# Mixing the experts' weights in bf16, column tile by column tile, with two positions in one column group

## The reference, cut to what matters

```python
x = jnp.transpose(hidden_states, (1, 0, 2))       # the 112 positions come first
h = jax.nn.relu(jnp.einsum('bsh,oh->bso', x, gW1) + gb1)
gate = jnp.einsum('bsh,eh->bse', h, gW2) + gb2
g = gate.mean(axis=1)                             # 112 x 8
W1 = jnp.einsum('be,eoi->boi', g, eW1)            # 112 matrices 1024 x 256
W2 = jnp.einsum('be,eoi->boi', g, eW2)            # 112 matrices 256 x 1024
y = jax.nn.relu(jnp.einsum('bsi,boi->bso', x, W1) + (g @ eb1)[:, None, :])
y = jnp.einsum('bsi,boi->bso', y, W2) + (g @ eb2)[:, None, :]
```

## Time and profile before

| | |
|---|---|
| median of 3 runs | 985.87 us (985.53 to 988.59) |
| the profiled execution | 978.81 us |
| its span, first to last instruction | 976.9 us |
| attention | 0 to 312 us |
| gates, residual, first chunk formed and used | 312 to 411 us |
| values of chunks 1 to 30 | 411.1 to 951.4 us |
| last chunk and output | 951.5 to 976.9 us |

### The profile page before, as it was taken

One profiled execution on the slowest core, in us unless ns is written; L12 is line 12 of the kernel. 1 busy time (PEld: TensorE's weight loads), 2 busy tenths in 40 slices (PEclk: granted clock), 3 DMA queues, 4 the chain that ended last, 5 costly groups with the idle time before them and its releaser, 6 DMA issues.

```text
span 976.9 us, 31690 instructions
## 1 busy us (share of the span) xinstructions
PE 843.7 (86%) x13150; PEld 545.8 (56%) x13150; DVE 556.1 (57%) x881; ACT 552.7 (57%) x852; POOL 216.6 (22%) x406
## 2 busy tenths in 40 slices
PE   2778899999987866199999999999999999999992
PEld 2657787877865423055555555555555555555552
DVE  6666667766664323056556556556556556565561
ACT  2536666767655335065665665665665655656650
POOL 7443555545522102320020020020020020020020
PEclk9889999999999857599999999999999999999997
DMA  6468666766650794523323223332233233222103
GB/s 184 109 169 206 181 157 176 173 170 166 167 146 13 196 124 90 157 71 109 89 68 108 89 87 89 88 96 86 83 108 90 82 95 89 93 84 67 45 2 77
DMA packets 114774, 109.38 MB, mean 112 GB/s; under 512 B 13434, under 2 KB 106842, under 8 KB 114658
## 3 DMA queue, kind: packets, MB, share of 16 engines
q1 hardware_dynamic: 114658, 107.67, 42.6%
HBM read 74.73 MB, written 32.75 MB: 110 GB/s over the span
## 4 chain that ended last, share of the span: by engine, by line
PE 59%; DMA 14%; ACT 10%; SPq 6%; DVE 3%; POOL 3%; issue 3%; ACTq 0%; POOLq 0%
PE banks L1601 25%; PE banks L1618 17%; ACT wb L962 9%; DMA k_stack<-k_dram 7%; PE banks L308 4%; PE banks L1445 4%; PE banks L1339 2%; PE banks L1298 2%; PE banks L1321 2%; DMA b_dram<-b_sb 2%; SPq L431 2%; DMA b_rows<-b_dram 2%; SPq L589 1%; DMA k_dram<-k_parts 1%; POOL y L723 1%
## 5 line engine op out<-in xcount | busy, mean ns | idle before, releaser
L962 ACT ACTIVATE wb<-banks 128x896 f32<-128x896 f32 x320 | 286.5, 916 | 242.4 <-PE banks L1601 232.6
L1601 PE MATMUL banks<-spread,ring 32*128 32x448 f32 x2048 | 274.6, 606 | 60.2 <-ACT wb L962 33.3
L1185 DVE COPY wb<-banks 128x896 f32<-128x896 f32 x192 | 209.5, 1091 | 203.5 <-PE banks L1601 190.2
L1601 PEld LDWEIGHTS banks<-spread,ring 32*128 32x128 f32 x2048 | 82.7, 188 | 129.4 <-ACT wb L962 92.0
L730 POOL TENSOR_SCALAR ht<-ht 128x256 f32<-128x256 f32 x64 | 47.8, 765 | 480.8 <-DVE ht L1209 478.7
L1618 PEld LDWEIGHTS banks<-wb,xt 128*32 128x32 f32 x3584 | 91.5, 111 | 85.8 <-DVE z L1199 26.7
L1057 DVE TENSOR_REDUCE maxima<-banks 112x2 f32<-112x750 f32 x128 | 117.7, 935 | 31.8 <-PE banks L1298 28.7
L1618 PE MATMUL banks<-wb,xt 128*32 128x128 f32 x3584 | 126.3, 279 | 0.0
L1618 PEld LDWEIGHTS banks<-wb,ht 128*32 128x32 f32 x3584 | 92.2, 109 | 59.1 <-DVE y L1199 48.7
L1618 PE MATMUL banks<-wb,ht 128*32 128x128 f32 x3584 | 116.9, 275 | 0.7 <-DVE y L1199 0.5
L765 ACT ACTIVATE probs<-banks 128x448 f32<-128x448 f32 x192 | 100.6, 544 | 28.5 <-PE banks L1321 26.3
(11 more groups left out here) (122 smaller groups left out, 847.2 us busy)
## 6 DMA issues: line engine op xcount, KB each, us to landing
w_nat<-in_w SPq DMA_DIRECT2D x64, 256.0 KB, 4.4
turned_dram<-w_turned SPq DMA_DIRECT2D x32, 512.0 KB, 3.1
ring<-turned_dram SPq DMA_DIRECT2D x32, 512.0 KB, 4.0
k_dram<-k_parts SPq DMA_DIRECT2D x16, 576.0 KB, 3.6
k_stack<-k_dram SPq DMA_DIRECT2D x32, 288.0 KB
k_stack<-k_dram SPq DMA_DIRECT2D x32, 192.0 KB
c_raw<-in_ctx_t SPq DMA_DIRECT2D x16, 375.0 KB, 5.3
y<-xmid_dram SPq DMA_DIRECT2D x8, 448.0 KB, 19.2
```

The costliest lines, as they stand in the source:

```text
L962: act.activation(wb[n % 2][:, :, at:at + 8].rearrange("p b (r k) -> p b r k", r=2), banks[:, bank:bank + 2, 0:4 * NQ].rearrange("p r (b k) ...
L1185: dve.tensor_copy(wb[n % 2][:, :, at:at + 8].rearrange("p b (r k) -> p b r k", r=2), banks[:, bank:bank + 2, 0:4 * NQ].rearrange("p r (b k ...
L1601: last = pe.matmul(banks[:, form_bank(half + r // 2, r % 2), 0:4 * NQ], ring[rows, n % 2, q, :], spread[rows].rearrange("p b k -> p (b k)" ...
```

## The change: what it does

- **Bf16 products.** Each fp32 weight and each fp32 gate is split into three bf16 parts (high, middle, low). Six products of parts, 8 experts x 2 each, are stacked in K: 96 rows. A form step is now a half (16 a chunk): 16 bf16 matmuls with a stationary of 96 x 32 (32 inputs) and a moving `spread` of 112 positions x 2 outputs = 224 columns, four side by side in four column groups. They are in the same 128 x 32 column tiling as the values.
- **Splitting.** PE transposes from `w_nat` with a step of eight elements. ACT copies the half to `w_split[:, 0]` as bf16 (`turned`), DVE subtracts it from PSUM into `w_rest` (`rest`), and when both halves are there POOL copies the middle part and subtracts the low part (`split`). SP writes 768 KB (`store_split`) and reads 1,536 KB back in twelve transfers of 16 partitions and 128 KB each (`load_ring`, two parts). `w_nat`, `w_split`, `w_rest` have one slot, and `ring` is two halves of one slot.
- **Pairs.** Two positions share a column group: `xt` and `ht` have a zero pad between the first position's 16 columns and the second's, and two matmuls accumulate, so `y` and `z` have 14 groups, not 28. Four units a chunk.
- **Order.** `ORDER` puts the second layer's chunks one chunk later; `hidden` now lies among the values of the next group's first chunk, except for the last group.
- **Copies out of PSUM.** `formed` reads PSUM with the four outputs innermost, 256 columns apart; before, four neighbouring columns were innermost.
- **Bias.** The bias of the second layer is made by matmuls (`mix_b2`) while chunk 0 is formed, and DVE adds it to `y` (`add_b2`).

```diff
-        DVE_HALVES = [(1, 1, 1, 0, 1, 1, 1, 0), (1,) * 8, (1, 1, 1, 0, 1, 1, 1, 0), (1, 0, 1, 0, 1, 0, 1, 0)]
+        ORDER = [("in", 0, 0), ("in", 0, 1)]
+        for i in range(OT - 1):
+            ORDER += [("in", i + 1, 0), ("out", i, 0), ("out", i, 1), ("in", i + 1, 1)]
+        ORDER += [("out", OT - 1, 0), ("out", OT - 1, 1)]
+        SIX, SEVEN = (1, 3, 6, 9, 11, 14), (1, 3, 5, 8, 10, 12, 14)
...
+        def period(n, form, turn, hidden, value):
+            form(n + 1, 0)
+            turn(n + TURN_AHEAD, 0)
+            form(n + 1, 1)
+            turn(n + TURN_AHEAD, 1)
+            done = 2
...
+            for g in range(GRP):
...
+                if done < HALVES:
+                    form(n + 1, done)
+                    done += 1
+                if i is not None and g == 0:
+                    hidden(i, 1)
+                value(n, g)
...
+        def formed(bank):
+            return (banks[:, bank:bank + 2, :].rearrange("p a (r c) -> p (a r) c", r=2)[:, :, 0:2 * NQ]
+                    .rearrange("p r (b k) -> p b k r", k=2))
...
 # SP
+            def store_split(m):
                 if turns_alive(m):
+                    sp.wait_ge(turn_low, m + 1)
+                    sp.dma_start(split_dram[m].rearrange("c p f -> p c f"),
+                                 w_split[:].rearrange("p c q i -> p c (q i)")).then_inc(turn_stored, 16)
+            def load_ring(m, part):
                 if turns_alive(m):
                     sp.wait_ge(turn_stored, 16 * (m + 1))
+                    need(sp, form_mm, HALVES * (m - 1) + HALVES // 2 * (part + 1))
+                    for k, piece in enumerate((0, 0, 0, 1, 1, 2)):
+                        src = split_dram[m, piece].rearrange("(r s) f -> r s f", s=8)
+                        sp.dma_start(ring[2 * E * k:2 * E * k + 2 * E, 4 * part:4 * part + 4, :],
+                                     src[:, 4 * part:4 * part + 4, :]).then_inc(ring_loaded[part], 16)
...
             for n in range(CHUNKS):
-                load_ring(n + 2)
-                store_turned(n + TURN_AHEAD)
-                load_natural(n + TURN_AHEAD + 2)
+                load_natural(n + TURN_AHEAD + 1)
+                store_split(n + TURN_AHEAD)
+                load_ring(n + 2, 0)
+                load_ring(n + 2, 1)
...
 # POOL
+            def split(m):
+                if turns_alive(m):
+                    pool.wait_ge(turn_rest, 2 * m + 2)
+                    need(pool, turn_stored, 16 * m)
+                    pool.tensor_copy(w_split[:, 1], w_rest[:]).then_inc(turn_mid, 1)
+                    pool.wait_ge(turn_mid, m + 1)
+                    pool.tensor_tensor(w_split[:, 2], w_rest[:], w_split[:, 1], ALU.subtract).then_inc(turn_low, 1)
...
 # ACT
+            def turned(m, w):
+                if turns_alive(m):
+                    act.wait_ge(turn_mm, 2 * m + w + 1)
+                    need(act, turn_stored, 16 * m)
+                    act.activation(w_split[:, 0, 4 * w:4 * w + 4, :].rearrange("p q i -> p (q i)"),
+                                   banks[:, turn_bank(m, w), :], ACT.Copy).then_inc(turn_high, 1)
...
 # DVE
+            def rest(m, w):
+                if turns_alive(m):
+                    dve.wait_ge(turn_high, 2 * m + w + 1)
+                    need(dve, turn_low, m)
+                    q = slice(4 * w, 4 * w + 4)
+                    dve.tensor_tensor(w_rest[:, q, :].rearrange("p q i -> p (q i)"), banks[:, turn_bank(m, w), :],
+                                      w_split[:, 0, q, :].rearrange("p q i -> p (q i)"), ALU.subtract)\
+                        .then_inc(turn_rest, 1)
...
+            dve.wait_ge(y_loaded, 16 * 8)
+            for q in range(HALVES):
+                taken_by_dve(0, q)
+                if q % 2 == 0 and q // 2 < GRP // 2:
+                    add_b2(q // 2)
...
 # PE
+            def form(n, q):
...
+                half = HALVES * n + q
+                half_taken(half - 3)
+                if q % (HALVES // 2) == 0:
+                    pe.wait_ge(ring_loaded[q // (HALVES // 2)], 16 * PRODUCTS * (n + 1))
...
                 for r in range(4):
+                    t = 4 * q + r
+                    for j in range(4):
+                        last = pe.matmul(banks[32 * j:32 * j + 32, form_bank(half) + r // 2, 256 * (r % 2):256 * (r % 2) + 2 * NQ],
+                                         ring[0:ROWS, t // 8, P * (t % 8) + 32 * j:P * (t % 8) + 32 * j + 32],
+                                         spread[0:ROWS].rearrange("p b k -> p (b k)"), start=True, stop=True)
                 last.then_inc(form_mm, 1)
...
+                m = g - UNIT_FROM[u]
+                for h in range(2):
                     for j in range(4):
+                        if ORDER[n][0] == "in":
+                            left = xt[:, ORDER[n][2], GRP * j + g, h:h + 2, :]
+                        else:
+                            left = ht[:, 4 * g + j, h:h + 2, :]
                         last = pe.matmul(banks[32 * j:32 * j + 32, 6 + v % 2, P * m:P * m + P],
+                                         left.rearrange("p h s -> p (h s)"), wb[n % 2][:, PAIRS * h + GRP * j + g, :],
+                                         start=(h == 0), stop=(h == 1))
```

More of the change, by code:

```diff
@@ L339, in turns_alive, with hidden_before @@
             return 0 <= m < CHUNKS
[L341 to L347, removed]
+        def hidden_before(n):
+            return n >= 2 and ORDER[n - 1][0] == "in" and ORDER[n - 1][2] == 1
@@ new lines, in unit_of @@
+        def unit_of(g):
+            return max(u for u in range(UNITS) if UNIT_FROM[u] <= g)
+        def period(n, form, turn, hidden, value):
[4 more added lines that the diff above has]
+            done = 2
+            i = ORDER[n - 1][1] if hidden_before(n) else None
+            if i is not None and ORDER[n][0] == "out":
+                for u in range(UNITS):
+                    form(n + 1, done)
+                    done += 1
+                    hidden(i, u)
+                i = None
+            for g in range(GRP):
+                if i is not None and g in UNIT_FROM[:3]:
+                    hidden(i, 0 if g == 0 else UNIT_FROM.index(g) + 1)
+                if done < HALVES:
+                    form(n + 1, done)
+                    done += 1
+                if i is not None and g == 0:
+                    hidden(i, 1)
+                value(n, g)
@@ L349, in build, with number @@
         UNIT, TAKEN = {}, []
         taken = {"act": 0, "dve": 0}
-        for n in range(CHUNKS):
[L352 to L356, removed]
+        def number(key, who):
+            UNIT[key] = len(TAKEN)
+            taken[who] += 1
+            TAKEN.append((who, taken[who]))
@@ new lines, in number_turn, with number_hidden, number_value, first_half @@
+        def number_turn(m, w):
+            if turns_alive(m):
+                UNIT["turn", m, w] = len(TAKEN)
+                TAKEN.append(("turn", 2 * m + w + 1))
+        def number_hidden(i, u):
+            number(("hidden", i, u), "dve")
+        def number_value(n, g):
+            if g in UNIT_FROM:
+                number(("value", n, unit_of(g)), "act" if first_half(n) else "dve")
+        def first_half(n):
+            return ORDER[n][0] == "in" and ORDER[n][2] == 0
+        for n in range(CHUNKS):
+            period(n, lambda n, q: None, number_turn, number_hidden, number_value)
@@ L365, in turn_unit, with unit_ready @@
             return UNIT["turn", m, w]
+        def unit_ready(eng, v):
+            eng.wait_ge(unit_mm, sum(who != "turn" for who, count in TAKEN[:v + 1]))
         def unit_taken(eng, v):
@@ L1137, in step @@
                     gate_sum(3)
+                    rest(0, 0)
+                    rest(0, 1)
+                if s.i is None and s.c == B + 1:
+                    rest(1, 0)
+                    rest(1, 1)
             dve.wait_ge(ones_set, 1)
```

492 lines of the change are left out of this document (240 added, 252 removed).

## The result

The changed kernel takes 1051.99 us (median of 4 runs, 1049.67 to 1056.24), the kernel before 987.1 us beside it: ratio 1.0662, 95% interval 1.0621 to 1.0704. The forecast was 968 us with a range to 1026. The profiled execution took 1049.67 us, its span is 1047.9 us.

A forecast was written before the change was run, and what follows sets the result against it. The DRAM chain was taken to bound each chunk: 16.7 us plus surcharges 0.6 and 0.4 made 17.7. Start 390, 29 chunks, 30 and 25.5 us gave a 959 us span; adding 9, 968 us, range 907 to 1026.

The forecast's parts named there:

- PE would be done at 14.6 or earlier: PE's work in a loop chunk: forms, values, turns and hidden sum to 14.3 us, 14.6 us with a wait.
- The ring's loads: Last link of the DRAM chain: six 128 KB transfers for the ring's first part, 5.5 us, between bounds 4.6 and 6.45.
- ring loads one behind the other: Rival at `load_ring`: a ring part takes 6.45 us, 19.0 us a chunk, 1005 us in all; chance 0.27.
- The chain's links: Between successive first forms: PE, ACT and DVE to 4.4 us, POOL 7.8, store 10.9, ring part and landing 16.7.
- the rule: Partitions 0 to 15 reach four of sixteen ports, some 104 GB/s: a ring part 7.5 us, kernel some 1035 us.
- Strided PSUM reads: Rival at `formed`'s copies: ACT's 0.92 to 1.66 us, DVE's 1.09 to 2.0; 19.3 us a chunk, 1014 us; chance 0.12.
- POOL's two operations: Chain term in `split`: middle part 1.1 us and low part 2.2 us, 3.4 us with the handover.
- The store: Chain term in `store_split`: 768 KB to DRAM, 3.1 us until its packets are out.
- The start: Ahead of the loop: residual to 375 us, then 13.6 us of copies and adds; first value near 390 us (380 to 400).
- Clock: Surcharge on the chain: 0.9 us where the clock falls after a wait, at about two chunks in three, so 0.6.
- The range: Whole kernel: 15.6 to 19.6 us a chunk, 5 us either way for the start, stated as 907 to 1026 us.
- the 17.7 forecast: Time of a loop chunk: chain of 16.7 us plus surcharges of 0.6 and 0.4, against 18.0 before.

The follow-up runs named there:

- e8: The changed kernel with the edits of e5 and e4 together: half the forming instructions and, from the third chunk on, 2 of 12 ring transfers; 898.19 us.
- e4: The changed kernel with instructions as they are, but ten of the twelve ring transfers left out from the third chunk on; 963.09 us.
- e5: The changed kernel with one forming matmul over 448 columns for two weight rows, 128 instead of 256 a chunk, same tiles and transfers; 1007.46 us, ratio 1.0244.
- e3: The changed kernel with two column tiles of 64 in place of four of 32 for forming, 128 matmuls a chunk; 1005.13 us.
- e1: The changed kernel with one full-width forming matmul over 128 columns in place of four over 32, 64 instead of 256 a chunk; 1003.35 us, ratio 1.0211.
- e12: e1 plus ring rows in every sixth partition, two forms then two value groups in turn, and chunk 0 formed ahead of the bias steps; 925.68 us, ratio 0.9408.
- e15: e12 with the first half of the ring load ahead of the store of the pieces in SP's queue; 913.85 us, ratio 0.9272.
- e9: The changed kernel with the same 12 ring transfers, each into every sixth partition instead of 16 neighbouring ones; 957.85 us.

## Why the prediction was wrong, step by step

- **"PE would be done at 14.6 or earlier" was right as work and wrong as time.** This is the step that failed. I priced the 16 x 4 form groups at 0.1 us each and the values as before, and never counted what PE must be given to run them. Form groups did come 0.1 us apart, and the work is 15.0 us a chunk in e8, with half of the forming instructions, and 15.6 in e4 beside its stops. But a packet of 16 KB serves 127 records and their weight loads. Without stops, the kernel after uses one up in (506.3 - 93.4) / 97 = 4.3 us, the kernel before in 448.7 / 61 = 7.4. At 4.3 us it stops for 1.0 us on average, at 5.6 us (e5, less its waits) for 0.2, at 6.4 us and more (e3, e1, before) for 0.02 or nothing. Beside a sixth of the ring's transfers 5.3 us were enough for 0.02 (e8). No rival of mine had this mechanism; the earlier trace rows held the count from which to ask.
- **The ring's loads: the rival's size, not mine.** I took 5.5 us for half a ring with 6.45 as the bound. The packets of a half take 5.5 to 7.4 us in the kernel after, 6.2 on average. The 172 GB/s that drew me to the middle weren't k_stack's alone: of the 0.76 MB of that stretch 0.59 were. In e5, where stops take only 0.5 us a chunk, the chunk is 18.8 us: the rival *ring loads one behind the other* (19.0). The chain's links were mine in part. SP's issues for a half's first part do stand behind the store's issue, and so behind POOL, in e12 (and e15 took that link away with its wait); in e1's chain the release of the half and the store's issue end within 0.2 us of each other; and in the kernel after only 10 of 25 stood directly behind the store, the others later, where the release of the half came last, which my sum left out. There this bound is hidden behind PE's stops, so its price did not show there as a wait. It showed through the fetches.
- **The Trainium skill's SBUF — State Buffer, "Door 1: The DMA port swizzle", speaks of exactly this.** By it 16 neighbouring partitions reach four of sixteen ports. In the kernel after, the ring's packets moved 131 GB/s with all engines busy (104 by that page of the Trainium skill), and a half's 0.786 MB in 6.2 us are 126. Every sixth partition, which by the table of the same page of the Trainium skill reaches thirteen or fourteen of the sixteen ports, gave packets of 0.44 us on average instead of 0.79. The trace agrees in kind. I had used the rule as a rival at the price of the transfer alone; the placement was worth 94 us. The row of the kernel after, one microsecond inside a ring half (length, busy times, granted clock, DMA share, GB/s):

```profile
640.00:641.00 1.00, 1.00 (x42) 0.80 (x38) 1.00 (x2) 1.00 (x2) 0.00 (x0) 1.00 1.01 131
```

- **Strided PSUM reads** cost nothing: 917 and 1086 ns, as before. POOL's two operations sum to 3.2 us (forecast 3.4 with the handover), `rest` is 0.685 us (0.69). The store lands in 4.6 us; I had its packets out in 3.1.
- **The start.** The natural block came at 347.2, y at 379.9 instead of 375 (SP issued it at 361.0, not 357), and chunk 0's forming took from there to 402 instead of 13.6 us. It is PE's: at a granted clock of 0.50 four bias matmuls take 2.07 us and two halves 1.6, together 3.6 us for each of the four full rounds.

```profile
384.50 1.68 PE L1704 MATMUL banks<-spread,ring 96*32 96x224 bf16 x32
386.12 2.07 PE L1751 MATMUL banks<-eb_sb,gate_wide 8*128 8x256 f32 x4
388.12 1.68 PE L1704 MATMUL banks<-spread,ring 96*32 96x224 bf16 x32
```

- **Clock.** I charged it 0.6 us a chunk for drops behind waits for the ring. The drops came behind the stops instead: 0.95 over the loop, 1.00 in e8.
- **The range** was added up wrongly: P from 15.6 to 19.6 with 5 us either way for the start gives 902 to 1028 us. 1052 is above that too.

What is shown: that the number of instructions matters with columns and bytes equal (e5, and e6 nearly so), that the ring's transfers make it worse with instructions equal (e4, e9), and that with both gone the chunk is 14.99 us, below the 17.7 forecast (e8). What is argued: that an instruction packet queues behind data packets in its DMA engine. For it speak the residual, during which PE had been dry for 5.2 us before the packet began (375.17 - 369.94), and the second and third of the four stops above, whose packets begin 1.0 us before and 0.6 behind the end of the ring's. Against a simple queue speaks the fourth, 2.5 us before that end, and that over the loop of the kernel after 30 of 97 instruction packets begin inside a ring half, more than 1.5 us before its end. When a packet is asked for is in no view. But the records bound it: if it is asked for when PE enters the block before (127 records back), it begins 1.1 to 5.5 us later in the kernel after (2.5 on average), and 10.1 us later ahead of the stop of 8.6. In e4 that distance is 1.25 us on average at the 14 stops where data held the engines less than half of it, and 2.5 at the 26 others. That would fit a packet which is asked for only one block ahead and held up by data; it is worked out from records, not tried. Nor was this kernel's one part tried on the kernel before (pairs without bf16).

## What to carry to other kernels

When an edit multiplies small matmuls, count instructions as well as columns: PE's work per 16 KB of its instructions is a quantity to check, and with 4.3 us of work per block, beside long transfers, PE ran dry. In a profile it looks like "issue" in the middle of a group that has no wait; the remedies were fewer, wider matmuls and shorter data transfers, and spreading a transfer's rows over the partitions cost nothing and gave most. An engine's own work, its supply and the transfers behind it have to be priced apart, since taking one away only shows the next (1052, 1007, 898 us).

## What the runs showed of the hardware that I had not expected

- PE's instructions come in packets of 16 KB, 256 to the packet, on a queue that the profile counts to the same 16 DMA engines as data. PE can stand still for 8.6 us while a 1.8 MB load of 14 KB packets runs.
- 16 rows of 8 KB into neighbouring partitions take 0.79 us a packet on average, into every sixth partition 0.44 us.
- A change between 128 x 32 fp32 and 96 x 128 bf16 tiles costs PE about 0.12 us.
- A load whose source is repeated over 3 groups of 16 partitions had two or three packets under way for 82% of its time, kept DMA at 35% and stretched the chunk to 26.5 us.
